# A graph-and-attention megakernel: the dense pass between its two edge sweeps is moved from group 4 of the third mixer layer to group 2, with the edge steps dealt out anew

## The reference

```
xn  = layernorm(x)
# graph branch, two convolutions one behind the other
conv(h, rel, W_in, W_out, W_loop, b):
    m   = h[src] * rel[edge_type]                 # gather two rows per edge, multiply
    agg = segment_sum(m @ (W_in | W_out) / deg, dst)
    return tanh(agg + h @ W_loop + b)
h1  = xn + res * conv(xn, rel1, ...)
h2  = h1 + res * conv(h1, rel2, ...)
gnn = h2 @ mu_w + mu_b
# mixer branch: 4 layers of linear attention and a 256-1024-256 gelu network on xn
for i in range(4):
    t = t + linear_attention(layernorm(t));  t = t + gelu(layernorm(t) @ W1 + b1) @ W2 + b2
x   = x + gnn + mixer(xn)
out = x + shared_mlp(layernorm(x)) + top-2 of 4 experts(layernorm(x))
```

## Time and profile before

| | |
|---|---|
| median of 3 runs | 2122.23 us (2119.59 to 2127.33) |
| the profiled execution | 2127.33 us, its span 2125.6 us |
| PE matmul busy | 1901.4 us (89% of the span) |
| POOL busy | 1335.1 us (63%) |
| DVE busy | 1262.3 us (59%) |
| ACT busy | 674.2 us (32%) |
| DMA | 371.60 MB, mean 175 GB/s |

### The profile page before, as it was taken

One profiled execution on the slowest core, in us unless ns is written; L12 is line 12 of the kernel. 1 busy time (PEld: TensorE's weight loads), 2 busy tenths in 40 slices (PEclk: granted clock), 3 DMA queues, 4 the chain that ended last, 5 costly groups with the idle time before them and its releaser, 6 DMA issues.

```text
span 2125.6 us, 31904 instructions
## 1 busy us (share of the span) xinstructions
PE 1901.4 (89%) x10496; PEld 1576.9 (74%) x10496; DVE 1262.3 (59%) x3298; ACT 674.2 (32%) x1858; POOL 1335.1 (63%) x1342
## 2 busy tenths in 40 slices
PE   3989899998999999889999897787988889889999
PEld 2568778886787788678888785556767777778898
DVE  7775466556556556665655654477545556446666
ACT  5533233343224334322433341121111111123443
POOL 4757777777777777767777227766767777730000
PEclk9999999999999999999999998899999999999999
DMA  8666666667766666766666346656655666660001
GB/s 213 191 205 208 202 190 199 199 189 223 223 200 192 196 200 189 220 208 197 196 199 213 98 132 191 207 189 195 196 180 182 197 190 190 188 125 18 5 22 37
DMA packets 191810, 371.60 MB, mean 175 GB/s; under 512 B 36589, under 2 KB 123035, under 8 KB 191656
## 3 DMA queue, kind: packets, MB, share of 16 engines
q0 software_dynamic: 78624, 225.58, 37.3%
q1 hardware_dynamic: 92986, 128.48, 18.7%
q10 hardware_dynamic: 20046, 15.57, 2.5%
HBM read 305.39 MB, written 64.95 MB: 174 GB/s over the span
## 4 chain that ended last, share of the span: by engine, by line
POOL 36%; PE 34%; issue 13%; DVE 7%; DMA 7%; SPq 2%; ACT 1%; DVEq 1%; ACTq 0%; POOLq 0%
POOL xg L823 23%; POOL rg L830 13%; PE ps_seg L2288 6%; PE ps_down L2411 5%; DMA xg<-h_rows,idx_tab 4%; PE ps_hid L2402 3%; PE ps_hid L2751 2%; DMA rg<-relation_rows,idx_tab 2%; SPq L633 2%; DVE xg L958 2%; PE ps_kv L2321 2%; PE ps_kv L2705 1%; PE ps_hid L496 1%; PE ps_down L2705 1%; PE ps_hid L2742 1%
## 5 line engine op out<-in xcount | busy, mean ns | idle before, releaser
L2288 PE MATMUL ps_seg<-xg,hot 128*125 128x257 f32 x1664 | 454.9, 402 | 131.9 <-DVE xg L958 131.3
L823 POOL DMA_INDIRECT xg<-h_rows,idx_tab x416 | 424.9, 1021 | 171.8 <-issue 114.3
L823 POOL DMA_INDIRECT xg<-xn_rows,idx_tab x416 | 430.8, 1036 | 158.6 <-issue 119.1
L830 POOL DMA_INDIRECT rg<-relation_rows,idx_tab x416 | 428.9, 1031 | 134.0 <-issue 126.1
L2288 PEld LDWEIGHTS ps_seg<-xg,hot 128*125 128x125 f32 x1664 | 297.5, 194 | 215.9 <-DVE xg L958 129.9
L958 DVE TENSOR_TENSOR xg<-xg,rg 128x512 f32<-128x512 f32 x416 | 286.6, 689 | 275.7 <-DMA xg<-h_rows,idx_tab 165.4
L2402 PEld LDWEIGHTS ps_hid<-hT,wff 128*128 128x128 f32 x3200 | 388.0, 194 | 16.3 <-issue 6.8
L2402 PE MATMUL ps_hid<-hT,wff 128*128 128x125 f32 x3200 | 391.5, 277 | 1.6 <-ACT gT L1945 0.9
L1945 ACT ACTIVATE gT<-ps_hid,b1p 128x125 f32<-128x125 f32 x800 | 225.9, 366 | 498.4 <-PE ps_hid L2402 498.1
L2411 PE MATMUL ps_down<-wff,gT 128*125 128x256 f32 x1600 | 369.4, 385 | 0.0
L2411 PEld LDWEIGHTS ps_down<-wff,gT 128*125 128x125 f32 x1600 | 300.6, 191 | 44.1
(11 more groups left out here) (364 smaller groups left out, 2392.8 us busy)
## 6 DMA issues: line engine op xcount, KB each, us to landing
second_relation_rows<-rg SPq DMA_DIRECT2D x104, 512.0 KB, 3.9
rg<-second_relation_rows SPq DMA_DIRECT2D x104, 512.0 KB, 3.8
wff<-L_mix_W ACTq DMA_DIRECT2D x8, 1024.0 KB, 8.5
xg<-xn_rows,idx_tab POOLq DMA_INDIRECT x416, 3.2
rg<-relation_rows,idx_tab POOLq DMA_INDIRECT x416, 3.4
xg<-h_rows,idx_tab POOLq DMA_INDIRECT x416, 3.5
h_rows<-rg SPq DMA_DIRECT2D x25, 112.0 KB
xres<-x POOLq DMA_DIRECT2D x5, 560.0 KB, 8.6
```

The source lines that it names most:

```text
L823: pool.indirect_dma_start(xg[:, k, 0:D], None, rows, bass.IndirectOffsetOnAxis(ap=idx_tab[:, step, 0:1], axis=0))\
L830: pool.indirect_dma_start(rg[:, k, :], None, rel_d, bass.IndirectOffsetOnAxis(ap=idx_tab[:, step, 1:2], axis=0))\
L2288: ins = pe.matmul(ps_seg[u // UW % 2][0:T, 0:AW], hot[:, s % RING, :], xg[:, s % RING, :], start=s % WIN == 0, stop=s % WIN == WIN - 1)
```

## The change

The dense pass is put at the start of iteration (2, 2) in place of (2, 4). So the first 416 steps are dealt over fewer stages, and the second 416 over more. Steps in each stage (a joint is J):

| | front | J0 | layer 0 | J1 | layer 1 | J2 | layer 2 | J3 | layer 3 |
|---|---|---|---|---|---|---|---|---|---|
| before | 24 | 14 | 20 28 26 26 26 | 14 | 20 28 26 26 26 | 14 | 20 26 26 26 / 92 | 36 | 60 60 60 60 48 |
| after | 40 | 18 | 28 26 28 26 28 | 18 | 28 26 28 26 28 | 18 | 26 24 / 52 60 60 | 24 | 44 44 44 44 44 |

The slash is the dense pass. The weights W_in and W_out have no buffer of their own any more; they are loaded over the transposed queries of group 1 (`qT_all[:, 5:10]`), and ACT waits ahead of that load until the attention of group 1 has read them.

```diff
-STEPS_FRONT = (0, 6, 6, 6, 6)
-STEPS_JOINT = (14, 14, 14, 36)
-STEPS_GROUP = ((20, 28, 26, 26, 26), (20, 28, 26, 26, 26), (20, 26, 26, 26, 92), (60, 60, 60, 60, 48))
-DENSE_LAYER, DENSE_GROUP = 2, 4
+STEPS_FRONT = (0, 10, 10, 10, 10)
+STEPS_JOINT = (18, 18, 18, 24)
+STEPS_GROUP = ((28, 26, 28, 26, 28), (28, 26, 28, 26, 28), (26, 24, 52, 60, 60), (44, 44, 44, 44, 44))
+DENSE_LAYER, DENSE_GROUP = 2, 2
...
-        in_q = sb("first_half_weights", [P, 2 * KC * D])
+        in_q = qT_all[:, GT:2 * GT, :].rearrange("p t n -> p (t n)")
...
                     if dense_behind(lay, gi):
 
+                        act.wait_ge(s_ao, (lay * NG + 2) * GT + 1)
                         load_graph(act, 0)
```

## The result

The changed kernel takes 2150.17 us in the median (2148.71 to 2154.56), the kernel before 2124.78 us over the same runs. The ratio is 1.0125 with a 95% interval of 1.0095 to 1.0154. The forecast was 2117 us, no clear change; the time lies 5 us above the upper end of its range (2145), near the rival "the second half starves" (2147).

What follows compares the result with a forecast made beforehand. POOL's gathers were taken to set both halves before, PE the second half after. First half 25 us saved, second half 20 us lost, dense pass and weight load 0: -5 us, giving 2117 us; range for 8 in 10, 2088 to 2145.

Steps and rivals of the forecast that it cites:

- the second half starves: Rival, second half: PE waits for steps, idle 7 us a stage; 50 us lost, 2147 us; chance 0.20.
- What bounds the kernel: Whole kernel: before, POOL's gathers set both halves; after, POOL leads the first and PE bounds the second.
- First half, 25 us saved: First convolution: 18 us from stalls, 4 from shorter gathers, 3 from PE's lag; bounds 10 and 33.
- Stalls: First half: of POOL's 22 us of waits for the ring, 4 stay in the joints and 18 are saved.
- shorter gathers: First half: two iterations' wide DVE operations, which lengthen gathers, leave; 2 us each, 4 us saved (0 to 6).
- The lag of PE: End of the first half: PE's last unit starts 5.3 us later than it could; 3 us taken back.
- the signs named: Changed profile: last gather near 1160 us, ring waits under 10 us, PE's share 86%, (1, 0) some 75 us.
- The moved weight load: Four transfers issued by ACT one whole iteration ahead, after a wait for group 1's attention already met: 0 us.
- the clock: Rival, first half: idle PE lowers its granted clock to 0.89, (x, 4) with joint takes 126 us; total 2127; chance 0.07.
- Second half, 20 us lost: First `up` behind the dense pass to the second dense pass: 629 us against 609.1; bounds 11 gained, 50 lost.
- the allowance for burstiness: Second half, each stage: added to the larger of PE and POOL, as in layer 3, 65 us with PE busy 63.5.

Runs made afterwards that it cites:

- doubling the supply: Changed kernel with POOL making only every other gather in the second convolution, PE's and DVE's work kept: 2327.8, 2296.2 and 2306.1 us in three runs.
- the even laying: Edge units placed evenly over PE's work inside second-half stages: 2123.1 us on the changed kernel (all but (2, 2)); 2113.3 us on the kernel before (layer 3 only).
- a later start: Changed kernel with edge units laid evenly, and those of (2, 2) placed later: 2124.8 us, 0.9992 of the kernel before.
- its stand-in: Changed kernel with W_in and W_out in their own buffer again and without ACT's added wait: 2391.0 us, 0.9991 of the kernel before.

## Why the prediction was wrong

- **What bounds the kernel** held: POOL in the first half, and PE's work per stage in the second. PE was forecast to be busy for 63.5 us of a layer-3 stage, or 61.4 without gaps inside the sums (the prediction does not show how it came to the second number); 61.8 to 63.0 us were measured.
- **First half, 25 us saved**: 30 measured, right in sign and size, but not by its parts. Stalls 18 forecast, 20 measured; shorter gathers 4 forecast, 12 measured (847.7 us busy for 832 gathers, before 859.7; 8 in a second trace). Of the 12 some 8 lie in the gathers that overlap the bias addition of L1118: 21 of them took 1.70 us in the mean before, and 23 took 1.28 after. So it was less the two iterations leaving than how the gathers fell beside those additions, which no part of the forecast had; that is luck. The lag of PE behind the last gather was to shrink by 3 and grew by 2 (its last unit starts 11.4 us after the gather's end, before 9.4). That more steps in the front would take its stalls away was wrong: by themselves they only moved them. Of the signs named, the ring's waits came to 9.6 us (under 10 forecast) and PE's busy share from 168 to 1100 us to 88% (86 forecast), but (1, 0) lasted 67.9 us and not 75.
- **The moved weight load and the clock** at nothing: no run speaks against it, though none measures the load. The granted clock of the changed kernel is 0.95 to 1.00 in its stages of the first half; (1, 4) with J2 lasted 121.4 us, not 126.
- **Second half, 20 us lost**: here the prediction failed. It lost 50. The failing step is the allowance for burstiness, stage by stage: (2, 2) 92.2 for 82, (2, 3) 91.5 for 87, (2, 4) with J3 138.4 for 134, layer 3 268.6 for 260, (3, 4) 69.7 for 66. In sum 31 us. The place was named (16 steps asked for in 14 us from a ring of 8), but for its price I took the 2 to 4 us that POOL lost when POOL alone was the bound. In a stage where PE's work and POOL's are near each other both sides pay: POOL's time with the ring full is not made up, as it has little slack, and PE's time with the ring empty is not either, as it has none. Two kinds of run bear this out by opposite means: doubling the supply takes 40 us off the half, and moving the units, with supply and work unchanged, takes 21 off, nearly all of it in layer 3.
- **How far that goes**: the even laying takes two thirds of the 31 us away, and not everywhere. Layer 3 then takes 246 us, 14 below its 260, while (2, 2) at 94.7 and (2, 4) with J3 at 140.5 stay 13 and 6.5 us above theirs. And as it shortens the kernel before as well, by 12 us in its second half (598.3 for 610.4), the changed one still loses some 40 us there with both laid evenly, against the 20 forecast. So the bursts explain about 10 of the 50 us between the two kernels as they stood. The rest goes with PE's added work, whose busy time in the half rises from 507 to 594 us, and with what stays open; the runs do not divide it further.
- **The rival "starves"** was right in sum, 50 us lost and 2147 us, and in layer 3 and (2, 3) as the place. Its price per stage in layer 3 was a little too high (68.5 us forecast, 67.2 in the mean) and made up for by (2, 2), 92.2 for 85: in part the sum came out by luck.
- **Open**: (2, 2). Of its 92.2 us PE is busy for 81.4 (79.6 forecast) and waits for steps for 9.9, in 7 pieces. With half of the gathers it still takes 87.8, 88.2 and 89.1 us, and the last of these has 4.5 us of such waits; a later start did not shorten it. The first gather behind the dense pass starts 4.3 us after the first `up`. What the rest is, and which way of laying this stage would help, is not settled. Open as well: (2, 4) with J3, and why on three chips every kernel's first half takes some 200 us more, with idle times on PE, ACT and DVE that their traces do not explain, and why the change then cost nothing (0.9991 for its stand-in).

## What to carry to other kernels

Work out a producer and a consumer that share a short ring by stages. Where their times come near each other (here 59 and 62 us), count the longest run in which the consumer takes nothing and the shortest in which it takes more than the ring holds: both can be lost time, and a producer that was held up needs its whole latency, here 6.3 us from the start of a unit's first gather to its multiplication, before it helps again. Before moving work between stages, look whether the hand-written places inside a stage are even over the consumer's own work; here that was worth 0.5% to the old kernel and 1.2% to the new one. Then compare like with like: with even laying in both, the move alone still costs 0.5%. The two kernels that beat the one before are the dense pass where it was with even laying (2113.3 us, 0.9947) and the dense pass at (2, 3) with even laying (2115.0 us, 0.9963); their intervals overlap.

## What the runs showed of the hardware that I had not expected

The mean of a gather's time on POOL in the first half went from 1.033 us to 1.019 us with the change, at the same median of 0.946 us; it was 1.020 to 1.024 us in three more traces with the dense pass at (2, 2), on the chips without the long first half. A gather that overlaps the bias addition of L1118 took 1.70 us in the mean before and 1.28 after. And one program can be 12% slower on one chip than on another (2126 and 2376 to 2395 us) with gathers at the same median (0.946 us), and most of the difference in the half with the most traffic.
